# Joining the q and k projections of an attention kernel: one projection, one bank per sequence, 512-wide splits

## The reference, cut to what matters

```
x = x + attention0(layernorm(x), ctx)   # 8 heads of 8, band |i-j| <= 64, softmax, then * ctx and a 64x64 mix
x = x + ffn0(layernorm(x))              # 256x256 ternary weights, norm and tanh
x = x + attention1(layernorm(x), ctx)   # q from x, k and v from ctx, rotary on q and k, full 256x256 softmax
x = x + ffn1(layernorm(x))              # 256 -> 1024 -> 256, 4-bit weights, LoRA
```

## Time and profile before

| what | value |
|---|---|
| median of 3 runs | 1358.52 us (1356.28 to 1361.82) |
| profiled execution: its own time | 1358.7 us |
| profiled execution: its span | 1356.8 us |
| PE busy over the span | 1268.8 us (94%) |
| DVE, ACT, POOL busy | 927.0, 852.3, 711.4 us |
| granted PE clock over the span | 0.982 of full speed |

### The profile page before, as it was taken

The page is one execution under the profiler, slowest core; times in us unless marked ns, Lnnn a source line. Parts: engine busy times, 40 slices in busy tenths (PEclk is TensorE's granted clock), DMA queues, the critical chain, the costliest instruction groups (busy, mean ns, idle before and its releaser), DMA issues.

```text
span 1356.8 us, 35892 instructions
## 1 busy us (share of the span) xinstructions
PE 1268.8 (94%) x10972; PEld 854.0 (63%) x10972; DVE 927.0 (68%) x2052; ACT 852.3 (63%) x1849; POOL 711.4 (52%) x1297
## 2 busy tenths in 40 slices
PE   6999999999999997868899999999999989999998
PEld 3677667777677764644566556666666646666665
DVE  6788888888888875549999978888888852111110
ACT  2576666666666765555888888888888772222111
POOL 4577778787777865045555656556655410100000
PEclk9999999999999999897999999999999999999999
DMA  8554444544445440023444434444444400000000
GB/s 202 117 132 102 114 113 112 111 109 111 111 102 120 100 96 7 12 52 92 90 99 102 105 88 100 97 102 110 98 97 102 105 6 0 31 16 15 15 15 31
DMA packets 90487, 113.33 MB, mean 84 GB/s; under 512 B 13972, under 2 KB 80276, under 8 KB 82740
## 3 DMA queue, kind: packets, MB, share of 16 engines
q1 hardware_dynamic: 89216, 111.25, 35.3%
q10 hardware_dynamic: 1206, 1.29, 0.4%
HBM read 18.66 MB, written 4.19 MB: 17 GB/s over the span
## 4 chain that ended last, share of the span: by engine, by line
PE 57%; POOL 16%; issue 10%; DVE 9%; ACT 3%; DMA 2%; POOLq 1%; SPq 0%; ACTq 0%; DVEq 0%
PE bank L475 9%; PE bank L435 8%; PE bank L678 8%; PE bank L669 8%; PE bank L451 8%; PE bank L433 5%; PE bank L487 4%; POOL probs L1340 4%; DVE row_max L1118 4%; POOL Qp L1311 2%; POOL rot L1322 2%; PE bank L627 1%; PE bank L507 1%; POOL k_rest L1327 1%; POOL q_rest L1307 1%
## 5 line engine op out<-in xcount | busy, mean ns | idle before, releaser
L1118 DVE TENSOR_REDUCE row_max<-bank 128x2 f32<-128x384 f32 (+1 forms) x1024 | 594.0, 616 | 109.9 <-PE bank L435 105.8
L714 ACT ACTIVATE probs<-bank 128x384 f32<-128x384 f32 (+1 forms) x1024 | 535.1, 542 | 182.9 <-PE bank L451 175.6
L435 PE MATMUL bank<-Ks,Qs 96*128 96x192 bf16 (+1 forms) x2048 | 372.2, 264 | 11.2 <-DMA Ks<-Ks 6.4
L451 PE MATMUL bank<-Qs,Ks 128*128 128x192 bf16 (+1 forms) x2048 | 366.0, 260 | 14.1 <-ACT probs L714 12.9
L1340 POOL TENSOR_SCALAR_AFFINE_SELECT probs<-probs 128x256 f32<-128x256 f32 (+1 forms) x512 | 260.9, 533 | 114.9 <-ACT probs L714 94.5
L435 PEld LDWEIGHTS bank<-Ks,Qs 96*128 96x128 bf16 x2048 | 187.9, 99 | 126.6 <-DVE row_max L1118 32.3
L475 PE MATMUL bank<-probs,V 128*32 128x192 f32 (+1 forms) x4096 | 248.2, 360 | 7.0 <-POOL probs L1340 5.7
L451 PEld LDWEIGHTS bank<-Qs,Ks 128*128 128x128 bf16 x2048 | 185.6, 97 | 48.2 <-ACT probs L714 34.5
L433 PE MATMUL bank<-band,ident 128*128 128x384 bf16 x512 | 168.7, 329 | 3.0 <-DMA Ks<-Ks 2.5
L475 PEld LDWEIGHTS bank<-probs,V 128*32 128x32 f32 x4096 | 107.4, 109 | 85.8 <-issue 43.9
L1277 DVE TENSOR_TENSOR X<-bank,X 128x256 f32 (+1 forms) x32 | 13.6, 424 | 185.6 <-PE bank L678 185.6
(11 more groups left out here) (118 smaller groups left out, 1675.3 us busy)
## 6 DMA issues: line engine op xcount, KB each, us to landing
Ks<-Ks SPq DMA_DIRECT2D x64, 576.0 KB
Qs<-Qs SPq DMA_DIRECT2D x128, 192.0 KB
Qs<-Qp SPq DMA_DIRECT2D x192, 64.0 KB
Ks<-Kp SPq DMA_DIRECT2D x192, 64.0 KB
side<-in_ctx SPq DMA_DIRECT2D x64, 128.0 KB, 2.1
X<-in_x SPq DMA_DIRECT2D x4, 1024.0 KB, 14.5
out<-X SPq DMA_DIRECT2D x8, 512.0 KB, 3.0
Qs<-max_rows SPq DMA_DIRECT2D x128, 12.0 KB
```

Source lines behind the costliest of these rows:

```text
L435: last = nc.tensor.matmul(dst[:, blk * win:(blk + 1) * win], Qs[0:SHIFT_ROW, pair[1], h, blk * P:(blk + 1) * P], Ks[0:SHIFT_ROW, pair[1], ...
L451: last = nc.tensor.matmul(dst[:, blk * win:(blk + 1) * win], Ks[:, pair[1], h, blk * P:(blk + 1) * P], Qs[:, pair[1], h, start(blk):start( ...
L714: nc.scalar.activation(probs[:, h % 8, 0:2 * win], exp_bank[h % 2][:, 0:2 * win], ACT.Exp, scale=SCALE).then_inc(s["exped"], 1)
L1118: nc.vector.tensor_reduce(row_max[:, pair[1], h, :], bank_of(pair, h)[:, 0:2 * win].rearrange("p (b k) -> p b k", b=2), AX.X, ALU.max).the ...
```

## The change

q and k of one sequence come out of one projection. The weights of q and k are interleaved column by column (q in even rows of the result, k in odd rows), so that one matmul over the 64 rows of one sequence gives 128 result rows. Sequence 0 goes to bank A, sequence 1 to bank B, both at h = 0 (`project_qk`). Layer 0 has two such matmuls for a pair; layer 1 has four, since q takes xn and k takes side (ctx), each with zeros for the other in its weights. ACT reads both banks at h = 1, DVE at h = 1 and 2. The buffers of q and k become one of 2 x 256 columns, and POOL's operations on them are 512 wide: in layer 0 two where there were four, in layer 1 five where there were ten. The moves into the stacks have the same bytes and half as many pieces of double the length, and the 16 heads stand in the order head, sequence. Two maximum jobs keep their places at h = 3 and h = 12. POOL's order in layer 1 is rot_sum, split, split_max half 0, split_max half 1. The diff, cut to its core:

```diff
-    "A": [("q", AHEAD), ("heads", -1), ("v", 2), ("max0", 1)],
-    "B": [("max1", 0), ("k", AHEAD), ("back", -1), ("out", -1), ("mix", -1)],
+    "A": [("qk", AHEAD), ("heads", -1), ("v", 2), ("max0", 1)],
+    "B": [("qk", AHEAD), ("max1", 0), ("back", -1), ("out", -1), ("mix", -1)],
...
+                    dst = bass.AP(q_stack, first + j * row, [[PARTS * row, HD], [2 * T, HEADS], [1, 2 * T]])
+                    e.dma_start(dst, QKp[0:P:2, u, j, :]).then_inc(s[f"q_in{u}"], 16)
                 for i in range(PARTS):
                     e.dma_start(Ks[COPY_ROW + i * HD:COPY_ROW + (i + 1) * HD, u, :, :],
-                                Kp[:, u, i, :]).then_inc(s[f"k_in{u}"], 16)
+                                QKp[1:P:2, u, i, :]).then_inc(s[f"k_in{u}"], 16)
...
+            def project_qk(pair):
+                if not active(pair):
+                    return
+                u = pair[1]
+                e.wait_ge(s["xn_ready"], num(pair) + 1)
+                if l:
+                    e.wait_ge(s[f"side_in{u}"], (pair[0] + 1) * 16)
+                wait_bank(e, s, l, "A", "qk", pair)
+                wait_bank(e, s, l, "B", "qk", pair)
+                sources = (xn, side) if l else (xn,)
+                for n, src in enumerate(sources):
+                    last = {}
+                    for bk, rows in (("A", slice(0, CH)), ("B", slice(CH, P))):
+                        last[bk] = nc.tensor.matmul(job_bank[bk][:, 0:T], w[rows, n, :], src[rows, u, :],
+                                                    start=(n == 0), stop=(n == len(sources) - 1))
+                last["A"].then_inc(s["A_filled"], 1)
+                last["B"].then_inc(s["B_filled"], 1)
...
                     if h == 3:
                         turn_max("B", r, 1)
-                    if h == 1:
-                        project("A", "q", p3, WQ, xn[:, p3[1], :],
-                                lambda: e.wait_ge(s["xn_ready"], num(p3) + 1))
-                    if h == 4 + l:
-                        project("B", "k", p3, WK,
-                                (side if l else xn)[:, p3[1], :],
-                                lambda: l and e.wait_ge(s[f"side_in{p3[1]}"], (p3[0] + 1) * 16))
+                    if h == 0:
+                        project_qk(p3)
...
+            def high_part(pair):
                 if not active(pair):
                     return
                 u = pair[1]
+                wait_some(e, s[f"q_in{u}"], pair[0] * PARTS * 16)
+                wait_some(e, s[f"k_in{u}"], pair[0] * PARTS * 16)
                 if l == 0:
+                    for seq, bk in enumerate("AB"):
+                        wait_job(e, s, l, bk, "qk", pair, "filled")
+                        nc.scalar.activation(QKp[:, u, 0, seq * T:(seq + 1) * T], job_bank[bk][:, 0:T], ACT.Identity,
+                                             bias=b[:, 0:1]).then_inc(s["qk_high"], 1)
                 else:
+                    e.wait_ge(s["rot_sum"], num(pair) + 1)
+                    nc.scalar.activation(QKp[:, u, 0, :], qk_rest[:, u, :], ACT.Copy).then_inc(s["qk_high"], 1)
...
+            def turn_rows(pair):
+                if not active(pair):
+                    return
+                wait_some(e, s["rot_sum"], num(pair))
                 half = P // 2
+                for seq, bk in enumerate("AB"):
+                    wait_job(e, s, l, bk, "qk", pair, "filled")
+                    for here, there in ((slice(0, half), slice(half, P)), (slice(half, P), slice(0, half))):
+                        nc.scalar.activation(rot[here, 1, seq * T:(seq + 1) * T], job_bank[bk][there, 0:T], ACT.Identity,
+                                             bias=b[there, 0:1]).then_inc(s["turned"], 1)
...
-                    if h == 2 and l == 0:
-                        high_part("A", "q", p3, Qp, 0)
-                    if h == 2 and l == 1:
-                        turn_rows("A", "q", p3, 0, 0)
+                    if h == 1 and l == 0:
+                        high_part(p3)
+                    if h == 1 and l == 1:
+                        turn_rows(p3)
                     if h == 3:
                         max_out("B", r, 1)
                     if h == VALUES_AT[l] + 1:
                         heads_out(m1)
-                    if h == 4 and l == 0:
-                        high_part("B", "k", p3, Kp, 1)
...
+            def rest_of(pair, seq):
+                if not active(pair):
+                    return
+                bk, here = "AB"[seq], slice(seq * T, (seq + 1) * T)
+                e.wait_ge(s["qk_high"], num(pair) * 2 + seq + 1)
+                wait_some(e, s["qk_parts"], num(pair) - RING + 1)
+                nc.vector.scalar_tensor_tensor(out=qk_rest[:, pair[1], here], in0=job_bank[bk][:, 0:T],
+                                               scalar=b[:, 0:1], in1=QKp[:, pair[1], 0, here],
                                                op0=ALU.add, op1=ALU.subtract).then_inc(s[f"{bk}_read"], 1)
...
-                    if h == 2 and l == 1:
-                        rotate("A", "q", p3, 0, 0)
-                    if h == 5 and l == 1:
-                        rotate("B", "k", p3, 1, 1)
-                    if h == 2 and l == 0:
-                        rest_of("A", "q", p3, Qp, q_rest, 0)
-                    if h == 4 and l == 0:
-                        rest_of("B", "k", p3, Kp, k_rest, 1)
+                    if h in (1, 2):
+                        (rotate if l else rest_of)(p3, h - 1)
...
+            def split(pair):
+                if not active(pair):
+                    return
+                u, n = pair[1], num(pair)
+                parts, rest, mid = QKp[:, u, :, :], qk_rest[:, u, :], s["qk_mid"]
                 if l == 0:
+                    wait_apart(e, job_wait(s, l, "A", "qk", pair, "read"), job_wait(s, l, "B", "qk", pair, "read"))
+                    total = 1
                 else:
+                    e.wait_ge(s["qk_high"], n + 1)
+                    nc.gpsimd.tensor_tensor(rest, rest, parts[:, 0, :], ALU.subtract).then_inc(mid, 1)
+                    wait_apart(e, (mid, n * 2 + 1))
+                    total = 2
+                nc.gpsimd.tensor_scalar(parts[:, 1, :], rest, 1.0, None, ALU.mult).then_inc(mid, 1)
+                e.wait_ge(mid, (n + 1) * total)
+                nc.gpsimd.tensor_tensor(parts[:, 2, :], rest, parts[:, 1, :],
+                                        ALU.subtract).then_inc(s["qk_parts"], 1)
...
+            def rot_sum(pair):
+                if not active(pair):
+                    return
+                e.wait_ge(s["turned"], num(pair) * 4 + 4)
+                turned = rot[:, 1, :].rearrange("p (s t) -> p s t", s=2)
+                nc.gpsimd.tensor_tensor(turned, turned, rope[:, 1, :].unsqueeze(1).broadcast_to([P, 2, T]),
                                         ALU.mult).then_inc(s["rot_mul"], 1)
+                wait_job(e, s, l, "A", "qk", pair, "read")
+                wait_job(e, s, l, "B", "qk", pair, "read")
+                e.wait_ge(s["rot_mul"], num(pair) + 1)
+                wait_some(e, s["qk_parts"], num(pair) - RING + 1)
+                nc.gpsimd.tensor_tensor(qk_rest[:, pair[1], :], rot[:, 0, :], rot[:, 1, :],
...
-                    split("q", p3, Qp, q_rest, "q_mid", "q_parts")
+                    split(p3)
...
-                    rot_sum("A", "q", p3, 0, q_rest)
-                    rot_sum("B", "k", p3, 1, k_rest)
-                    split("q", p3, Qp, q_rest, "q_mid", "q_parts")
+                    rot_sum(p3)
+                    split(p3)
                     split_max(e, nc.gpsimd, s, l, p1, 0)
-                    split("k", p3, Kp, k_rest, "k_mid", "k_parts")
                     split_max(e, nc.gpsimd, s, l, p1, 1)
```

155 lines of the change are left out of this document (56 added, 99 removed).

## The result

The changed kernel takes 1529.88 us (median of 4 runs, 1528.12 to 1530.38) against 1358.74 us for the kernel before (1356.28 to 1361.82). The ratio is 1.125, with a 95% interval of 1.124 to 1.127. The forecast was 1500, with a range of 1440 to 1545.

A forecast was written before the change was run, and what follows sets the result against it. PE's own in-order stream was taken to set the end, so every wait inside an iteration adds time. 1358.7 us plus 70 for layer 0 and 73 for layer 1 gave 1501.7, about 1500, range 1440 to 1545.

The forecast's parts named there:

- bank B in layer 0: Maximum job at h = 3 waits for DVE's second read of the projection, starting 4.7 us after it; net +1.7 us.
- bank B in layer 1: Maximum job waits for DVE's second rotate, starting 4.85 us into the iteration where it was 2.85; PE waits 1.35 us.
- bank A in layer 1: Maximum job at h = 12 waits 1.5 us for POOL's late split, starting at 14.5 us into the iteration.
- PE's own work: Row halves of the joined projection run side by side: 0.65 us in layer 0, 1.07 in layer 1.
- The rival without overlap: Row halves run one after the other, 0.46 us more in layer 0, 0.92 in layer 1: 1540 us, chance 0.12.
- the one in which only the bank waits bite: Rival: POOL's wide operations cost hardly more than narrow ones or its lateness is hidden; 1444 us, chance 0.10.
- Layer 1, +73: Layer 1 loses 2.7 us in each of 29 iterations, 78 us, less 5 for waits already paid.
- Layer 0, +70: Layer 0 loses 2.4 us in each of 29 iterations, from the bank B wait and POOL's late mask.
- 1.7 us for bank B: Layer 0, net loss per iteration from the late maximum job at h = 3, after k's 0.53 us is taken off.
- 0.7 for a V product that waits for POOL: Layer 0, POOL's mask behind the 512-wide split ends at 8.8 us, the V product needs it at 8.1.
- the forecast's own bounds: 1465 to 1525 us for the whole kernel: POOL's wide operations 10% either way, the joined projection at its bounds.
- Slack 9 us: Last DMA into the stacks is issued 9 us before it is needed; job and need move together, so no cost.

The follow-up runs named there:

- Experiments 1 and 2: Changed kernel with layer 0's joined projections in q's and k's old slots, 1447.63 us; with layer 1's half-0 maximum split ahead of POOL's wide split, 1492.35; both, 1408.37.
- 5: Kernel before, q and k apart and operations 256 wide, but with the changed kernel's order on every engine: 1564.33 us.
- experiment 3: Changed kernel with each sequence's joined projection in q's and k's old slots in both layers, plus POOL's early maximum split in layer 1: 1403.52 us.
- filler_half: Changed kernel with 7 unneeded matmuls on PE ahead of layer 0's late maximum job: 1503.38 us.
- The two fillers: Changed kernel with unneeded matmuls on PE ahead of layer 0's late maximum job: 14 of them 1506.54 us, 7 of them 1503.38 us.
- experiment 6: Changed kernel with the joined projection at h = 7 and three arrangements of the reads, split and moves behind it: 1517.39, 1673.63 and 1560.04 us.
- experiment 7: Kernel before with one line moved in layer 1, POOL's split of the half-0 maxima ahead of the split of q: 1350.11 us.
- experiment 4: Changed kernel with 14 or 7 unneeded matmuls filling PE's gap ahead of layer 0's late maximum job: 1506.54 and 1503.38 us.

## Why the prediction was right, and where its numbers were off

**Three waits, and their places: right.** They were where the prediction put them: bank B in layer 0 at 4.72 us after the projection (forecast 4.7), bank B in layer 1 at 5.19 with a wait of 1.34 (4.85 and 1.35), bank A in layer 1 with a wait of 1.27, 14.6 us after the iteration's start (1.5 and 14.5). Experiments 1 and 2 show that taking away the first and the last gives back what they cost, and 5 that they come from the order and not from the joined form. The second went in experiment 3, but what it cost is known only together with the longer projection.

**PE's own work: right.** Two row halves take 0.63 us in layer 0 (0.65) and 1.07 in layer 1 (1.07). The rival without overlap is out, and so is the one in which only the bank waits bite: POOL's order alone gave 37.5 us.

**Layer 1, +73: right.** The stretch measured +75, a steady iteration 17.94 (17.8).

**Layer 0, +70: one term held, one did not.** The stretch measured +90; at full clock, in filler_half, it is +66. The sum had 1.7 us for bank B and 0.7 for a V product that waits for POOL. The first held: over the middle of the layer (90 to 480 us) the job starts 4.80 us after the iteration does, where it was 2.49; less k's 0.53 that is 1.8. The second isn't there: PE waits for POOL at no V product, in the changed kernel as in filler_half. In one iteration of the changed kernel POOL's wide split ended at 332.51 and the next mask then waited 0.83 for ACT, which was late with PE itself. In its place come small delays behind the late job. In filler_half the way from the job to the next projection takes 13.26 us on the mean, and in the kernel before it was 13.03, less k's 0.53. So 0.75 where 0.7 stood, of which the list of waits names 0.4 (5.3 us for ACT at the heads' transposition, 3.4 for DVE at a score, in 21 iterations); the rest is open. The size of this term is right by luck, not by its reason.

**The clock: missing.** A wait was priced as its own length. In layer 0 each one of 2.4 us or more also brought 3.4 us or more at half speed, 96 us in the middle of the layer. The two fillers put this at 23 and 26 us for the kernel, and at 24 in the stretch of layer 0. The difference to the forecast of 1501.7 then comes out as -4 in layer 0 at full clock, +24 for the clock, +2 in layer 1, and +7 at the layers' edges (+5, +2).

**The range: held by a rival that was wrong.** 1529.88 lies above the forecast's own bounds (1465 to 1525). It is within 1440 to 1545 only because the range took in the rival without overlap of row halves, and that is not what happened.

**A part of the reasoning on hidden work was thin.** "Slack 9 us" for the stacks held for this change, since need and issue moved together. It was taken as nearly free in experiment 6, where 6.0 of the 9 turned out to be the time from the issue to the released matmul.

**Still open.** Whether a joined projection can cost less than the 1350 us of experiment 7. It was tried at h = 0, in the two old slots, and at h = 7 with three arrangements of the work behind it; each turned up another wait or cost. A maximum job with its own columns in bank B, which would not have to wait for the read of the projection, was not tried.

## What to carry to other kernels

When two jobs share a bank, price a new order by who stands behind each read, on every engine: here two projections that cost PE 0.36 us less an iteration (0.63 for 0.99) made it 3.4 longer. Of that 1.8 is the late read behind two maxima and 1.0 the clock that fell behind the wait. Price an idle gap of TensorE not by its length alone, but look at the granted clock behind it; if it can't be closed, work put into half of it can be enough (experiment 4). And look for the small urgent operation that stands behind a long one in the same queue: putting it first was worth 37 us in the changed kernel and 9 in the tuned one.
